# Two transformer blocks on one core: mask first in the second scores, V projections from fp16 halves, new stage order

## What is computed

```
xn = layernorm(x)                  # block 0
x  = x + attention0(xn) + experts(xn)
     # attention0: 16 heads of 16, ALiBi slopes, causal mask, softmax, max(., 1e-10), output projection
     # experts: sum over 8 of w_e * ((silu(xn Wg_e) * (xn Wu_e)) Wd_e), w_e from sigmoid(xn Wr)
xn = layernorm(x)                  # block 1
x  = x + attention1(xn) + ffn1(xn)
     # attention1: 16 heads, causal softmax, biases
     # ffn1: ternary W1 (1024x256), gelu, ternary W2, then 4-bit quantisation
     #       with one scale, max|y|/7, over all batches
```

## Time and profile before

| | |
|---|---|
| time, median of 3 runs | 839.89 us (839.71 to 840.85) |
| the profiled execution | 839.0 us, of which its span is 837.3 us |
| TensorE matmuls / weight loads | 695.7 us (83%) / 502.6 us |
| VectorE | 578.1 us (69%) |
| ScalarE | 478.3 us (57%) |
| GpSimd | 228.6 us (27%) |
| mean granted TensorE clock | 0.927 of full |

### The profile page before, as it was taken

The page is one execution under the profiler, slowest core; times in us unless marked ns, Lnnn a source line. Parts: engine busy times, 40 slices in busy tenths (PEclk is TensorE's granted clock), DMA queues, the critical chain, the costliest instruction groups (busy, mean ns, idle before and its releaser), DMA issues.

```text
span 837.3 us, 19783 instructions
## 1 busy us (share of the span) xinstructions
PE 695.7 (83%) x6519; PEld 502.6 (60%) x6519; DVE 578.1 (69%) x2197; ACT 478.3 (57%) x1237; POOL 228.6 (27%) x260
## 2 busy tenths in 40 slices
PE   0576667889888997889898997989898998999775
PEld 0454445667565775667575775767565776677533
DVE  3579867786587747795587747786587748786454
ACT  2457654945388355955388354945378354953533
POOL 6945441231113121231113121231113121132223
PEclk9879898999989999999989997999979999999868
DMA  6733012200303030201202030200303030300362
...
DMA packets 49544, 57.10 MB, mean 68 GB/s; under 512 B 5056, under 2 KB 40000, under 8 KB 49472
## 3 DMA queue, kind: packets, MB, share of 16 engines
...
## 4 chain that ended last, share of the span: by engine, by line
PE 61%; DVE 14%; ACT 8%; issue 8%; DMA 5%; ACTq 1%; SPq 1%; POOL 1%; DVEq 1%; POOLq 0%
PE gen_ps L1084 15%; PE gen_ps L1095 8%; PE value_ps L1202 7%; PE gen_ps L1058 5%; PE gen_ps L1126 3%; PE gen_ps L1070 3%; DVE probs L1461 3%; PE gen_ps L1115 3%; PE value_ps L1208 3%; PE turn_ps L1177 2%; PE score_ps L1139 2%; ACT hid L950 2%; PE turn_ps L1168 2%; DMA gu_lo<-x_dram 1%; PE turn_ps L1149 1%
## 5 line engine op out<-in xcount | busy, mean ns | idle before, releaser
L962 ACT ACTIVATE probs<-probs,nmax 128x256 f32<-128x256 f32 (+1 forms) x256 | 113.4, 445 | 57.8 <-DVE nmax L1461 57.3
L820 POOL TENSOR_TENSOR h_lo<-hid,h_hi 128x512 f16<-128x512 f32 x64 | 76.6, 1197 | 204.8 <-ACT h_hi L943 204.8
L1084 PE MATMUL gen_ps<-xe_hi,gu_hi 128*128 128x256 f16 x512 | 103.3, 285 | 8.4 <-DVE gated L1407 4.3
L1461 DVE CUSTOM_DVE_ANT_0 probs<-score_ps,bias 128x256 f32<-128x256 f32 (+1 forms) x256 | 80.5, 352 | 35.4 <-PE score_ps L1141 24.6
L1084 PE MATMUL gen_ps<-xe_lo,gu_hi 128*128 128x256 f16 x512 | 102.2, 283 | 0.0
L1475 DVE CUSTOM_DVE_ANT_0 junk<-score_ps,bias 128x256 bf16<-128x256 f32 (+1 forms) x256 | 76.1, 354 | 37.3 <-PE score_ps L1141 33.3
L1084 PE MATMUL gen_ps<-xe_hi,gu_lo 128*128 128x256 f16 x512 | 101.8, 282 | 0.0
L990 ACT ACTIVATE et<-turn_ps 128x384 f32<-128x384 f32 x128 | 55.8, 488 | 69.0 <-PE turn_ps L1177 69.0
L1486 DVE TENSOR_SCALAR probs<-probs,rsum 128x256 f32<-128x256 f32 (+1 forms) x256 | 81.3, 360 | 4.6
L1139 PE MATMUL score_ps<-k_stack,q_stack 64*128 64x256 f16 x256 | 37.7, 291 | 46.0 <-DVE nmax L1461 36.2
L971 ACT ACTIVATE pt<-turn_ps 128x384 f32<-128x384 f32 x128 | 61.2, 480 | 23.4 <-PE turn_ps L1151 23.4
...
## 6 DMA issues: line engine op xcount, KB each, us to landing
...
```

The costliest lines, as they stand in the source:

```text
L820: pool.tensor_tensor(h0_lo[:, e], hid0[:, e], h0_hi[:, e], ALU.subtract).then_inc(s_h0l, 1)
L962: last = act.activation(probs[:, k, lo:hi], probs[:, k, lo:hi], ACT.Exp, scale=-1.0, bias=nmax[:, k, j:j + 1], accum_out=esum[:, k, j:j + 1])
L1084: last = pe.matmul(g[:, S * f:S * f + S], w[:, st.arg, m, k, cols], xx[:, k, :], start=(i == 0), stop=(i == len(terms) - 1))
L1461: last = dve.tensor_tensor_reduce(out=probs[:, k, lo:hi], in0=g[:, lo:hi], in1=bias0[:, s, blo:S], scale=-1.0, scalar=BIG, op0=ALU.add, op ...
```

## The change

1. `s`: the mask is added by the first pair of matmuls (start=True) and the maximum by the last (stop=True); the eight matmuls are the same.
2. `v0`, `v1`: six fp16 matmuls in place of two fp32 ones, from xt_hi, xt_lo and weights split into halves in new stages `vsplit:0`, `vsplit:1` (one ScalarE and one VectorE instruction each). xt is no longer made. V is 16 times larger: vb is scaled by 16, the tile of ones holds 16, the router's tanh and the copy of the values are scaled back.
3. In the first batch the normalised x goes into `acc`, not over x0; ln0b no longer waits for the sum with the output bias, and GpSimd adds that bias after it has computed the reciprocal deviation and issued its weight loads.
4. Bias tiles: the second GpSimd instruction for each four heads is a selection on the half that has masked places, in place of an addition over all.
5. New order lists and new LAG tables.

With the LAGs worked in, VectorE's queue at the top of a pass is score:0 ln1a score:1 norm:0 ln1b gate:0 score:2 rt1 up:0 norm:1 tr1 score:3 (before: ... gate:0 rt1 up:0 score:2 tr1 score:3 norm:1), and ScalarE's at the end is m:0 s:0 quant:0 s:1 quant:1 quant:2 quant:3 s:2 s:3 m:1 quant:4 s:4 (before: m:0 quant:0 quant:1 s:0 quant:2 s:1 s:2 quant:3 quant:4 s:3 m:1 quant:5 s:4).

```diff
--- before.py
+++ after.py
@@ LAG, the shifts of stages in the ScalarE and VectorE queues @@
...
 FIRST_ORDER = """
-    setup:0 ln0a split:1 xe split:0 ln0b split:3 tr0 setup:2 split:2 v0:0 q0 l0 k0 setup:1 split:5 rt1 gate:0 v0:1
-    split:4 up:0 gate:1 rt2 split:7 split:6 down:0 up:1 0 1 gate:2 2 down:1 3 up:2 split:8 gate:3 4 5 split:9 up:3
-    down:2 tern:0 split:10 6 tmx:0 tern:1 split:11 gate:4 7 down:3 8 9 up:4 10 11 12 tern:2 gate:5 down:4 tern:3 13
-    split:13 +ln0a split:12 up:5 tern:4 tsm:0 tern:5 gate:6 14 up:6 gate:7 +ln0b 15 tern:6 up:7 16 down:5 tmx:1 tern:7
-    17 +tr0 18 tern:8 down:6 +q0 +k0 tern:9 +v0:0 19 +v0:1 +xe +l0 tsm:1 tern:10 tern:11 down:7 op0
+    ln0a split:1 setup:0 xe split:0 ln0b split:3 tr0 setup:2 split:2 vsplit:0 q0 l0 k0 gate:0 setup:1 split:4 rt1 v0:1
+    split:5 v0:0 up:0 gate:1 0 rt2 split:7 down:0 split:6 up:1 1 gate:2 2 down:1 3 4 up:2 split:8 gate:3 5 split:9
+    up:3 down:2 tern:0 6 split:10 tmx:0 7 tern:1 split:11 gate:4 down:3 8 9 up:4 10 11 12 tern:2 gate:5 down:4 tern:3
+    13 split:13 +ln0a up:5 split:12 tsm:0 tern:4 tern:5 gate:6 14 up:6 gate:7 +ln0b vsplit:1 down:5 15 tern:6 up:7 16
+    tmx:1 tern:7 +tr0 17 tern:8 down:6 +q0 18 +k0 tern:9 +v0:0 19 +v0:1 +xe +l0 tsm:1 tern:10 tern:11 op0 down:7
 """
 STEADY_ORDER = """
-    0 ln1a 1 ln1b gate:0 up:0 rt1 2 tr1 3 rt2 q1 k1 4 down:0 5 gate:1 6 up:1 7 gate:2 v1 w1:3 w1:0 w1:1 w1:2 l1 8 h1:0
-    up:2 9 10 h1:1 down:1 11 h1:2 gate:3 b:1 h1:3 up:3 down:2 12 13 14 15 b:0 16 gate:4 b:3 17 mp:0 up:4 b:4 18 down:3
-    b:2 +ln0a mp:1 w2 b:5 m:0 19 s:1 gate:5 op0 +ln0b s:0 b:6 +tr0 gate:6 up:5 down:4 s:2 +q0 b:7 y:0 s:3 +k0 up:6 +l0
-    +xe y:1 m:1 down:5 s:4 gate:7 +v0:0 s:5 up:7 s:6 y:2 s:7 down:7 y:3 +v0:1 down:6 op1
+    0 ln1a 1 ln1b gate:0 2 up:0 rt1 tr1 3 rt2 q1 4 k1 down:0 5 gate:1 6 up:1 7 gate:2 w1:3 w1:0 l1 8 w1:1 w1:2 v1 h1:0
+    up:2 9 gate:3 10 h1:1 down:1 11 h1:2 b:1 h1:3 up:3 12 down:2 13 14 15 b:0 16 gate:4 b:3 17 mp:0 up:4 b:4 18 +ln0a
+    mp:1 down:3 w2 b:2 19 m:0 down:4 s:1 b:5 op0 gate:5 +ln0b s:0 b:6 +tr0 gate:6 up:5 s:2 b:7 y:0 +q0 s:3 +k0 up:6
+    +l0 +xe y:1 m:1 down:5 s:4 gate:7 s:5 +v0:0 up:7 s:6 y:2 s:7 down:7 y:3 +v0:1 down:6 op1
 """
 LAST_ORDER = """
-    ln1a gate:0 rt1 0 ln1b rt2 1 tr1 2 gate:1 up:0 3 q1 k1 4 down:0 5 up:1 6 gate:2 v1 w1:1 w1:2 w1:0 w1:3 l1 7 up:2 8
-    h1:1 down:1 9 gate:3 10 11 12 h1:0 h1:3 13 b:0 up:3 14 down:2 15 h1:2 b:1 gate:4 16 up:4 b:4 gate:5 17 18 b:3
-    down:3 19 b:2 mp:0 up:5 down:4 b:5 gate:6 up:6 b:7 m:0 gate:7 s:2 b:6 down:5 mp:1 up:7 s:0 down:6 op0 down:7 s:1
-    +ln1a y:0 s:3 m:1 +ln1b w2 +tr1 s:4 y:1 +q1 +k1 s:5 s:6 +l1 y:2 s:7 +w1:0 y:3 +w1:1 +w1:2 +w1:3 op1
+    ln1a gate:0 rt1 0 rt2 ln1b 1 tr1 2 gate:1 up:0 3 q1 k1 4 down:0 5 up:1 6 gate:2 v1 h1:1 w1:1 w1:2 w1:0 w1:3 l1 7
+    up:2 8 gate:3 down:1 9 10 11 12 h1:3 h1:0 13 b:0 up:3 14 down:2 15 h1:2 b:1 gate:4 16 up:4 b:4 17 18 gate:5 b:3
+    down:3 up:5 b:2 19 mp:0 down:4 b:5 gate:6 up:6 b:7 m:0 mp:1 gate:7 s:2 b:6 down:5 up:7 s:0 down:6 op0 down:7 s:1
+    +ln1a y:0 s:3 m:1 +ln1b w2 +tr1 s:4 y:1 +q1 +k1 s:5 s:6 +l1 y:2 s:7 +w1:0 y:3 +w1:1 +w1:3 +w1:2 op1
 """
 FINAL_ORDER = """
-    b:0 h1:1 b:1 h1:0 h1:3 h1:2 b:2 v1 fetch b:7 w2 b:3 mp:0 qmax m:0 b:4 quant:5 mp:1 quant:2 s:3 quant:0 b:6 b:5 s:1
-    s:0 quant:1 quant:3 y:0 s:2 m:1 quant:7 s:4 y:1 s:5 s:6 quant:4 y:3 s:7 quant:6 y:2 op1
+    h1:0 h1:1 b:1 h1:3 h1:2 v1 b:2 b:0 b:7 w2 b:3 m:0 s:3 mp:0 qmax fetch mp:1 b:4 quant:2 s:1 quant:5 quant:0 b:6 b:5
+    quant:1 s:0 y:0 s:2 m:1 s:5 quant:7 quant:3 y:1 s:4 s:6 quant:4 y:3 s:7 quant:6 y:2 op1
 """
...
-        wv_sb = [sb("wv0_sb", [P, NK, D + E]), sb("wv1_sb", [P, NK, D])]
+        wv_hi = [sb("wv0_hi", [P, NK, D + E], F16), sb("wv1_hi", [P, NK, D], F16)]
+        wv_lo = [sb("wv0_lo", [P, NK, D + E], F16), sb("wv1_lo", [P, NK, D], F16)]
...
-        xt = sb("xt", [P, NK, S])
...
+        et_flat = et[:].rearrange("p s q -> p (s q)")
+        wv_raw = [et_flat[:, 0:NK * (D + E)], et_flat[:, NK * (D + E):NK * (2 * D + E)]]
...
+                if n.reg is None and n.off == 1:
+                    sp.wait_ge(s_xb[0], NT)
...
-                pool.memset(ones[:, C:2 * C], 1.0).then_inc(s_tab, 1)
+                pool.memset(ones[:, C:2 * C], WSCALE).then_inc(s_tab, 1)
...
-                    if st.kind == "first":
-                        pool.wait_ge(s_ob, 32)
...
-                    for t in range(NT):
-                        pool.tensor_tensor(total[:, t], src[:, t], ob[l][:], ALU.add).then_inc(s_xb[l], 1)
+                    def add_bias():
+                        for t in range(NT):
+                            pool.tensor_tensor(total[:, t], src[:, t], ob[l][:], ALU.add).then_inc(s_xb[l], 1)
+
+                    early = st.kind == "first" and n.off == 0
+                    if not early:
+                        add_bias()
...
                     wait(pool, s_st[l], n.at(5, 5))
                     pool.tensor_tensor(rstd[l][:], var[l][:], minus_half[:], ALU.pow).then_inc(s_rstd[l], 1)
-                    if st.kind == "first" and n.off == 0:
+                    if early:
                         load_weights()
+                        pool.wait_ge(s_ob, 32)
+                        add_bias()
...
-                        pool.tensor_tensor(bias0[:, four], bias0[:, four], bias1[:].unsqueeze(1).broadcast_to(shape), ALU.add)\
-                            .then_inc(s_bias, 1)
+                        pool.affine_select(out=bias0[:, four, P:S], in_=bias0[:, four, P:S], compare_op=ALU.is_ge, fill=MASKED,
+                                           base=0, pattern=[[0, 4], [-1, P]], channel_multiplier=1).then_inc(s_bias, 1)
...
+            for l, w in enumerate((wv0, wv1)):
+                act.dma_start(wv_raw[l].rearrange("p (k n) -> p k n", k=NK),
+                              w.rearrange("(k p) n -> p k n", p=P)).then_inc(s_wv[l], 16)
...
+                if name == "vsplit":
+                    act.wait_ge(s_wv[st.arg], 16)
+                    act.activation(wv_hi[st.arg][:].rearrange("p k n -> p (k n)"), wv_raw[st.arg], ACT.Copy, scale=WSCALE)\
+                       .then_inc(s_vhi, 1)
...
-                    act.activation(xt[:].rearrange("p k s -> p (k s)"), g[:, :], ACT.Copy).then_inc(s_xh[l], 1)
...
+                    act.activation(at[0][:, g], value_ps[:, 0:S], ACT.Copy, scale=1.0 / WSCALE).then_inc(s_at[0], 1)
...
-                    src = (x0, acc)[l]
+                    src = acc if first else (x0, acc)[l]
...
-                        for k in range(NK):
-                            last = pe.matmul(o, xt[:, k, P * t:P * t + P], wv_sb[l][:, k, :],
-                                             start=(k == 0), stop=(k == NK - 1))
+                        terms = [(xx, w, k) for xx, w in ((xt_hi, wv_hi), (xt_lo, wv_hi), (xt_hi, wv_lo)) for k in range(NK)]
+                        for i, (xx, w, k) in enumerate(terms):
+                            last = pe.matmul(o, xx[:, k, P * t:P * t + P], w[l][:, k, :],
+                                             start=(i == 0), stop=(i == len(terms) - 1))
...
-                        pe.matmul(turn_ps[hp][:, P:3 * P], k[rows[hp], i, 0:P], q[rows[hp], i, :], start=True, stop=False,
+                        pe.matmul(turn_ps[hp][:, 0:2 * P], ident_b[:], later_b[:].rearrange("p t q -> p (t q)"),
+                                  start=True, stop=False, skip_group_check=True)
+                    for hp in range(2):
+                        pe.matmul(turn_ps[hp][:, P:3 * P], k[rows[hp], i, 0:P], q[rows[hp], i, :], start=False, stop=False,
                                   skip_group_check=True)
                     for hp in range(2):
                         pe.matmul(turn_ps[hp][:, 0:P], k[rows[hp], i, P:S], q[rows[hp], i, P:S], start=False, stop=False,
                                   skip_group_check=True)
                     for hp in range(2):
-                        pe.matmul(turn_ps[hp][:, 0:3 * P], pick[rows[hp], i, :], max_row[rows[hp], :], start=False, stop=False,
-                                  skip_group_check=True)
-                    for hp in range(2):
-                        pe.matmul(turn_ps[hp][:, 0:2 * P], ident_b[:], later_b[:].rearrange("p t q -> p (t q)"),
-                                  start=False, stop=True, skip_group_check=True).then_inc(s_tn[1], 1)
+                        pe.matmul(turn_ps[hp][:, 0:3 * P], pick[rows[hp], i, :], max_row[rows[hp], :], start=False, stop=True,
+                                  skip_group_check=True).then_inc(s_tn[1], 1)
...
+                    for l in range(2):
+                        dve.tensor_scalar(vb[l][:], vb[l][:], WSCALE, None, ALU.mult).then_inc(s_set, 1)
...
+                if name == "vsplit":
+                    dve.wait_ge(s_vhi, st.arg + 1)
+                    dve.scalar_tensor_tensor(wv_lo[st.arg][:].rearrange("p k n -> p (k n)"), wv_raw[st.arg], WSCALE,
```

(19 more changed lines are left out.)

15 lines of the change are left out of this document (7 added, 8 removed), and 54 rows, old and new, of the table LAG.

## The result

The changed kernel takes 803.1 us, the median of four runs (800.6 to 807.9); the kernel before took 839.9 us beside it. The ratio is 0.957, with a 95% interval from 0.952 to 0.962. Twice more, beside other kernels, the same changed kernel took 810.3 and 807.5 us, with ratios of 0.964 and 0.959 (intervals 0.960 to 0.967 and 0.954 to 0.963). So the gain is 32 to 37 us, where 20 were forecast.

A forecast was written before the change was run, and what follows sets the result against it. TensorE, busy 83% of the span, was taken as the bound. Six middle passes -10, last pass -0.5, start -5, end -4.5 gave -20 us from 839.0: 819, or 820 us against the median; range 808 to 836 us.

The forecast's parts named there:

- the -1.7 us of a middle pass: Sum for each of six middle passes: -2.0 reordered first half, +0.5 later q1, -0.2 V projections; -10 us in all.
- V's price: V projections, fp16 for fp32: 0.83 us a batch less matmul time, of which only 0.2 us a pass counted.
- (a): Top of a middle pass: score:2 before up:0, hole 4.25 us instead of 2.94, q1 0.5 us later.
- (b): Middle pass: w1:0 and w1:1 before v1, score:8 earlier, gate:3 fills the 1.01 us hole before score:10; value:1 no earlier.
- (c): Middle pass: down:2 behind score:12, its additions behind score:13; the 2.09 us hole before score:14 shrinks to a few tenths.
- The gap at value:1: Middle pass: ScalarE's full queue keeps value:1 from coming earlier, so the hole before it grows to about 1.4 us.
- The second half at nothing: Reordered second half of a middle pass: costed at nothing, bounds 0 and +0.5 us a pass.
- The mask at nothing: Second scores with the mask first, 64 stages: taken as nothing, or 0.1 us either way each, 6 us in all.
- The start: Selection for bias tiles, early normalising, new first order: -5 us at the first steady pass, bounds -8 and 0.
- Rival C: Longer hole at the top of a pass keeps TensorE at the low 1.2 GHz clock: slower, 848 us; chance 0.06.
- Rival B: Reordering a pass brings nothing; only projections, start and end count: -11 us, 829 us; chance 0.22.
- D: Start, end and the moves (b) and (c) gain nothing, projections offset by tr1's delay: 840 us; chance 0.07.

The follow-up runs named there:

- e8: The kernel before with fp16 V projections and the new orders and LAG tables, without early normalising, bias tiles by selection and mask first: 813.6 us, ratio 0.969.
- e1: The kernel before with only the V projections from fp16 halves, the copy xt gone; old orders, LAG tables and start: 833.3 us, ratio 0.992.
- e9: The changed kernel with V in fp32 again and GpSimd's subtraction for the second block's low halves cut to 4 of 256 columns: 814.4 us, ratio 0.973.
- e12: The changed kernel with the top of the middle pass ordered as before, changed LAG tables kept: 807.3 us, beside 807.5 for the changed kernel.
- e7: The kernel before with 24 matmuls that compute nothing before score:2 and 24 before q1 in each of the six middle passes: 826.5 us, ratio 0.987.
- e13: The changed kernel with the middle of the middle pass ordered as before, V in fp16, changed LAG tables kept: 830.1 us, ratio 0.986.
- e14: The changed kernel with the second half of the middle pass ordered as before, changed LAG tables kept: 809.0 us, beside 807.5 for the changed kernel.
- e4: The kernel before with only the first batch normalised into acc ahead of the bias additions and the bias tiles masked by selection: 844.9 us, ratio 1.002.
- e3: The changed kernel with V in fp32 again, xt copied again and no split stages: 827.6 us, ratio 0.983.

## Why the prediction was wrong

The sign held, the size didn't, and the miss lies in one place. Against the profile before, "first" came 7.0, 2.5 and 5.1 us earlier in the three profiles of the changed kernel (forecast 5), "rest" is 6.6, 5.8 and 5.2 us shorter (forecast 0.5 + 4.5), and the six passes 20.5, 20.2 and 19.6 us (forecast 10). The failed term is the -1.7 us of a middle pass, which measured -3.4. What was wrong in it is that it priced the removed holes by their length alone and had no term for the clock. Its 10 us were 6.3 of waits, 3.7 of work and nothing of clock; e8, with V and the orders alone, has 4.9 us less of waits, 4.0 less of work and 12.4 less of clock than the kernel before.

- **V's price** held: 0.83 us a batch forecast, and e1's six passes have 4.9 us less work, 0.82 each. What failed is "It doesn't": I counted 0.2 us a pass and v1's 0.41 as covered. Alone, V gave 9.2 us in the six passes, 5.3 of them in the clock's column; in the new order and without the collision it gave nothing (e9).
- **(a), the top**: the wait of 4.25 us came, split in two, and q1 is 0.48 us later behind op1 (12.68 to 13.16 us; forecast 0.5). Yet putting the top back (e12) gained nothing: the six passes are 546.0 us against 547.2, where my term wanted 3 us back. So the delay of q1 did not reach the time, as far as e12 with the changed LAG tables can show it.
- **(b) and (c), the middle**: the step that failed. The holes of the earlier trace rows went nearly as forecast, from 3.8 us a pass to 1.9 to 2.7 in the first five passes of the changed kernel, and with V in fp32 and no collision (e9) the waits of the six passes are 6.2 us shorter, where the moves and the later q1 together had 6.5 in the forecast (six times 2.0 less v1's 0.41 less 0.5). What the -2.0 us left out is the clock: its cost fell by 12.4 us in e8 and 12.3 in e9, and by 5.5 to 8.8 in the changed kernel. By e7, where 12.4 of 21.6 us reached the time, that is worth an estimated 7 us in e8 and 4 in the changed kernel, of the 10 us missed. A collision that comes and goes with the order is the second thing the sum could not see. That the moves alone are worth 3.8 us a pass, as e13 might say, isn't shown, since e13 makes a collision of its own.
- **The gap at value:1**: 1.4 us forecast, 0.70 measured. ScalarE's full stretch was no hard floor: value:1 starts 24.44 us after q1 instead of 25.07, and 24.03 in e7, which has the order of the kernel before.
- **The second half at nothing** held within the noise of the time: e14 is 1.5 us slower. In the six passes it is 2.4 to 3.3 us slower, so the new second half gains 0.4 to 0.5 us a pass there, where my bounds had only a loss of up to 0.5.
- **The mask at nothing, bounds 6 us either way**: in line with the six passes, which differ by under 2 us with the mask first or last.
- **The start**: the size held, the division didn't. Selection and early normalising alone gave nothing (e4); in the new order they may be worth what e8's "first" of 162.8 is above 156.6 to 161.1, some 2 to 6 us, though "first" moves by 4.5 us by itself. The selection took 1.04 us each, 0.9 was taken.
- **Rival C**, slower by the clock: the condition came (4.25 us of waits at the top, and the low level in a stretch of 3.4 us behind it from 223.2), but the low time fell, 61 us before against 38 to 44 in the six passes. Its mechanism is real, with the other sign: e7 shows 21.6 us of the clock's cost hanging on the waits of the kernel before. I had this price in my hands, "each us of busy low clock costs half a us", used it for the loss and not for the gain. The holes I removed should have been given a clock term.
- **Rival B** fell: the orders took 12.1 us from the six passes when V was already in fp16 (e1 to e8). D fell too.

By the table the 20.1 us of the passes (mean of three profiles) are 8.6 of work, 4.5 of waits and 7.1 of clock. Of the 8.6 of work V is 4.9; the other 3.7 are the hint at the mask's place, which e8 does without at the same time.

**What stays open**: how the 10 us divide exactly, with one profile of the kernel before and a clock that moves by itself; and why fp32 V puts three normalisations a pass beside GpSimd's subtractions in the new order and fp16 V puts none there. e3 and e9 show what it costs, not what sets the phase; v1's 0.4 us and the copy of 0.6 us on ScalarE are both candidates, not tried apart.
